# Linear attention and FP4 feed-forward: attention output turned on VectorE and through device memory in place of TensorE

## What is computed

```python
q = _split_heads(x @ Wq); k = _split_heads(x @ Wk); v = _split_heads(x @ Wv)   # 16 heads of 64
q = jax.nn.relu(q) + EPS
k = jax.nn.relu(k) + EPS
context = jnp.cumsum(jnp.einsum('bhnd,bhne->bhnde', k, v), axis=2)
D_inv = 1.0 / jnp.einsum('bhnd,bhnd->bhn', jnp.cumsum(k, axis=2), q)
attn = jnp.einsum('bhnd,bhnde,bhn->bhne', q, context, D_inv)
return attn.transpose(0, 2, 1, 3).reshape(b, n, H * DH) @ Wo + bo
...
x = x + attention(_layernorm(x)); x = x + ffn(_layernorm(x))
```

## Time and profile before

| | us |
|---|---|
| runs, median (lowest to highest) | 1593.6 (1592.9 to 1594.48) |
| profiled execution, span of its instructions | 1592.7 |
| PE busy | 1575.6 |
| DVE busy | 1118.9 |
| ACT busy | 672.7 |
| POOL busy | 477.8 |

### The profile page before, as it was taken

One profiled execution on the slowest core, in us unless ns is written; L12 is line 12 of the kernel. 1 busy time (PEld: TensorE's weight loads), 2 busy tenths in 40 slices (PEclk: granted clock), 3 DMA queues, 4 the chain that ended last, 5 costly groups with the idle time before them and its releaser, 6 DMA issues.

```text
span 1592.7 us, 55490 instructions
## 1 busy us (share of the span) xinstructions
PE 1575.6 (99%) x24464; PEld 1485.6 (93%) x24464; DVE 1118.9 (70%) x2438; ACT 672.7 (42%) x1281; POOL 477.8 (30%) x706
## 2 busy tenths in 40 slices
PE   8999999999999999999999999999999999999998
PEld 6999999999999999999999999999999999999998
DVE  7886766666766667666667666676666666666767
ACT  5444344444444434444344443434434344443433
POOL 3332323323233223232232333222322323322233
PEclk9999999999999999999999999999999999999999
DMA  4100000000000000000000000000000000000000
GB/s 161 33 2 16 16 15 5 15 13 15 15 6 15 12 16 16 15 5 16 12 16 15 6 15 12 16 15 16 5 15 12 16 15 6 15 12 16 9 6 18
DMA packets 22013, 26.82 MB, mean 17 GB/s; under 512 B 1808, under 2 KB 20752, under 8 KB 21776
## 3 DMA queue, kind: packets, MB, share of 16 engines
q1 hardware_dynamic: 21776, 23.27, 4.6%
HBM read 14.88 MB, written 8.39 MB: 15 GB/s over the span
## 4 chain that ended last, share of the span: by engine, by line
PE 94%; DVE 4%; issue 1%; DMA 1%; ACT 0%; SPq 0%; POOL 0%; DVEq 0%; POOLq 0%; ACTq 0%
PE bank L496 66%; PE bank L760 3%; PE bank L629 3%; PE bank L664 3%; PE bank L618 3%; PE bank L580 3%; PE bank L805 3%; PE bank L700 3%; PE bank L727 1%; PE bank L747 1%; PE bank L778 1%; PE bank L602 1%; PE bank L506 1%; DMA qkT<-in_L_attn_Wk 1%; PE bank L739 0%
## 5 line engine op out<-in xcount | busy, mean ns | idle before, releaser
L1011 ACT ACTIVATE qkT<-bank 128x512 f32<-128x512 f32 x256 | 153.0, 599 | 275.9 <-PE bank L496 223.6
L1380 POOL TENSOR_SCALAR qkT<-qkT 128x512 f32<-128x512 f32 x256 | 187.9, 741 | 266.2 <-ACT qkT L1011 266.2
L496 PE MATMUL bank<-xT_hi,wqk_hi 128*128 128x256 f32 x1024 | 213.4, 289 | 0.3 <-DVE wqk_lo L1467 0.3
L496 PE MATMUL bank<-xT_hi,wqk_lo 128*128 128x256 f32 x1024 | 203.1, 279 | 0.0
L496 PE MATMUL bank<-xT_lo,wqk_hi 128*128 128x256 f32 x1024 | 203.1, 279 | 0.0
L1350 POOL TENSOR_TENSOR rstd<-var,minus_half 128x1 f32<-128x1 f32 x64 | 35.6, 556 | 430.3 <-DVE var L1664 430.3
L496 PEld LDWEIGHTS bank<-xT_hi,wqk_hi 128*128 128x128 f32 x1024 | 155.2, 188 | 3.9 <-DVE wqk_lo L1467 0.8
L496 PEld LDWEIGHTS bank<-xT_lo,wqk_hi 128*128 128x128 f32 x1024 | 156.1, 188 | 0.0
L496 PEld LDWEIGHTS bank<-xT_hi,wqk_lo 128*128 128x128 f32 x1024 | 156.0, 188 | 0.0
L1467 DVE TENSOR_TENSOR hqT_lo<-bank,hqT_hi 128x512 fp32r<-128x512 f32 x120 | 63.7, 552 | 118.7 <-ACT hqT_hi L1087 118.7
L1467 DVE TENSOR_TENSOR attnT_lo<-bank,attnT_hi 128x512 fp32r<-128x512 f32 (+1 forms) x128 | 88.0, 689 | 60.8 <-ACT attnT_hi L1078 60.3
(11 more groups left out here) (213 smaller groups left out, 3947.2 us busy)
## 6 DMA issues: line engine op xcount, KB each, us to landing
x_in<-in_L_attn_x SPq DMA_DIRECT2D x32, 256.0 KB, 2.7
out<-out_sb SPq DMA_DIRECT2D x64, 128.0 KB, 1.7
qkT<-in_L_attn_Wq SPq DMA_DIRECT2D x1, 1024.0 KB, 8.7
qkT<-in_L_attn_Wk SPq DMA_DIRECT2D x1, 1024.0 KB, 10.9
probs<-in_L_attn_Wv SPq DMA_DIRECT2D x1, 512.0 KB, 3.5
k_tok<-in_L_attn_Wv SPq DMA_DIRECT2D x1, 512.0 KB, 6.1
attn<-in_L_attn_Wo SPq DMA_DIRECT2D x1, 512.0 KB, 12.1
x<-in_L_attn_Wo SPq DMA_DIRECT2D x1, 512.0 KB, 13.1
```

The lines of the kernel that those rows point to most:

```text
L496: at = pe.matmul(dst, lhs_at(kt), rhs_at(kt), start=first and kt == 0, stop=last and kt == k_tiles - 1)
L1011: act.activation(flat(qkT[:, 2 * m:2 * m + 2, :]), bank[bank_of["qk", c, n]][:], ACT.Relu).then_inc(qk_relu, 1)
L1380: pool.tensor_scalar(at, at, QK_EPS, 1.0, ALU.add, ALU.mult).then_inc(qk_ready, 1)
```

## The change

For chunks 4 to 61 PE no longer turns the attention output. DVE turns it in blocks of 32x32 (`block_attn`, one instruction over 128x1024, from `attn` to `probs`, whose scores are used up by then). Three DMAs store the blocks to device memory (the odd tiles' halves swapped) and four DMAs fetch them back into `attn`, so that the blocks come to lie in turned order. ACT then rounds the tile to the high part in one instruction, and the low part, a subtraction of the whole tile, moves from DVE to POOL. The order of the eight slices in `attnT_hi` changes, and the output product takes them by `attn_slot`.

For even chunks among them (`is_late`) the output product moves to the next step, right behind its attention; with it `add_x`, `variance`, `begin_x`, `end_x` and their partners on ACT and POOL. For odd chunks the product stays at the end of the step, and the high and low parts stand behind the q/k tile n = 5. `mask` now waits until the stores have read `probs`, `normalize` until the low part of the chunk before has read `attn`.

```diff
+    GROUP = 32
+    GROUPS = P // GROUP
+    SENT_ATTN = range(CHUNKS, END)
+        attn_away = nc.dram_tensor("attn_away", (P, INNER), F32, kind="Internal").ap()
...
+        def attn_slot(n, kt):
+            return kt % 2 * (KI // 2) + kt // 2 if n in SENT_ATTN else kt
+        def is_late(n):
+            return n in SENT_ATTN and n % 2 == 0
+        attn_raw = attn[:].rearrange("p (i k c) -> p i k c", i=GROUPS, c=GROUP)
+        attn_blocks = probs[:, 0:INNER].rearrange("p (a o e) -> p a o e", a=GROUPS, o=2)
+        def by_raw_attn(t):
+            return t[:].rearrange("p k (i c) -> p i k c", c=GROUP)
...
+            def send_attn(n):
+                sp.wait_ge(attn_blocks_ready, sent_attn(n) + 1)
+                if sent_attn(n):
+                    sp.wait_ge(attn_back, 16 * GROUPS * sent_attn(n))
+                to = attn_away.rearrange("p (a o e) -> p a o e", a=GROUPS, o=2)
+                sp.dma_start(to[:, :, 0, :], attn_blocks[:, :, 0, :]).then_inc(attn_sent, 16)
+                for half in range(2):
+                    here, there = (slice(DH * k, DH * (k + 1)) for k in (half, 1 - half))
+                    sp.dma_start(to[there, :, 1, :], attn_blocks[here, :, 1, :]).then_inc(attn_sent, 16)
+            def fetch_attn(n):
+                sp.wait_ge(attn_sent, 48 * (sent_attn(n) + 1))
+                at = attn_away.rearrange("(i r) (a e) -> a r i e", r=GROUP, a=GROUPS)
+                for a in range(GROUPS):
+                    sp.dma_start(attn[GROUP * a:GROUP * (a + 1), :].rearrange("r (i e) -> r i e", i=GROUPS), at[a]
+                                 ).then_inc(attn_back, 16)
             def step(b, c):
...
+                if g in SENT_ATTN:
+                    send_attn(g)
+                    fetch_attn(g)
...
                 else:
                     last_attend(b, c, g, u)
+                if is_late(g - 1):
+                    project_out(*divmod(g - 1, CHUNKS), g - 1)
...
-                    turn_attn(b, c, g, n)
+                    if g not in SENT_ATTN:
+                        turn_attn(b, c, g, n)
...
-                project_out(b, c, g)
+                if not is_late(g):
+                    project_out(b, c, g)
...
+            def high_sent_attn(n):
+                act.wait_ge(attn_back, 16 * GROUPS * (sent_attn(n) + 1))
+                act.wait_ge(wo_done, n)
+                act.activation(by_raw_attn(attnT_hi), attn_raw, ACT.Copy).then_inc(attnT_hi_ready, 2)
...
-                if normed:
+                if normed and not is_late(g - 1):
                     normalize_x2(g - 1)
                 evacuate_v(c, u + 1, c % 2, 1 - c // 2)
+                if is_late(g - 1):
+                    high_sent_attn(g - 1)
...
                         relu_qk(c, u + 1, 2 * n)
+                        if n == 0 and is_late(g - 1):
+                            normalize_x2(g - 1)
                         relu_qk(c, u + 1, 2 * n + 1)
+                        if n == 1 and is_late(g - 1):
+                            square_x(g - 1)
...
                         relu_qk(c, u + 1, n)
+                        if n == 5 and c % 2 == 1 and g in SENT_ATTN:
+                            high_sent_attn(g)
...
+            def low_sent_attn(n):
+                pool.wait_ge(attnT_hi_ready, 2 * (n + 1))
+                pool.tensor_tensor(by_raw_attn(attnT_lo), attn_raw, by_raw_attn(attnT_hi).bitcast(F32), ALU.subtract
+                                   ).then_inc(attnT_ready, 2)
...
+                late = is_late(g - 1)
+                if late:
+                    low_sent_attn(g - 1)
...
+                if late:
+                    scale_h(g - 3)
...
+                    add_eps(u + 1, 0)
+                    if late:
+                        rstd_2(g - 1)
+                    for n in range(1, 4):
                         add_eps(u + 1, n)
+                    if late:
+                        scale_x(g - 1)
                     for n in range(4, 6):
                         add_eps(u + 1, n)
+                    if g in SENT_ATTN:
+                        low_sent_attn(g)
...
             def mask(g, n):
+                if n == 0 and g - 1 in SENT_ATTN:
+                    dve.wait_ge(attn_sent, 48 * sent_attn(g))
...
+                if n == 2 and g != LAST:
+                    dve.wait_ge(state_ready, (CHUNKS - 1) * b + c)
...
+                if half == 0 and g - 1 in SENT_ATTN:
+                    dve.wait_ge(attnT_ready, 2 * g)
+            def block_attn(g):
+                dve.wait_ge(attn_ready, 2 * (g + 1))
+                dve.transpose(attn_blocks.rearrange("p a o (k c) -> p o k a c", c=GROUP),
+                              attn[:].rearrange("p (k o a c) -> p o k a c", o=2, a=GROUPS, c=GROUP)
+                              ).then_inc(attn_blocks_ready, 1)
...
                     normalize(g, 0)
                     normalize(g, 1)
+                if g in SENT_ATTN:
+                    block_attn(g)
+                if is_late(g - 1):
+                    add_x(g - 1)
+                    variance(g - 1)
+                if is_late(g - 1):
+                    begin_x(g - 1)
...
+                    if half == 0 and is_late(g - 1):
+                        end_x(g - 1)
+                    if g not in SENT_ATTN:
+                        low_attn(g, half)
...
-                add_x(g)
+                if not is_late(g):
+                    add_x(g)
```

More of the change, by code:

```diff
@@ L206, in build_program @@
         attn_copied, hq_copied = sem("attn_copied"), sem("hq_copied")
+        attn_blocks_ready, attn_sent, attn_back = (
+            sem("attn_blocks_ready"), sem("attn_sent"), sem("attn_back"))
         down_done, out_ready = sem("down_done"), sem("out_ready")
@@ L402, in x2_of, with sent_attn, turned_attn @@
             return x_bias[1][:, 1, :] if n == LAST else x2[:, n % CHUNKS, :]
+        def sent_attn(n):
+            return len(range(SENT_ATTN.start, min(max(n, SENT_ATTN.start), SENT_ATTN.stop)))
+        def turned_attn(n):
+            return n - sent_attn(n)
+        def attn_slot(n, kt):
[6 more added lines that the diff above has]
+            return t[:].rearrange("p k (i c) -> p i k c", c=GROUP)
         def as_rows(t, k):
@@ L767, in project_out @@
                 pe.wait_ge(attnT_hi_ready, 2 * (g + 1))
-                product(dst, lambda kt: attnT_hi[:, kt, :], lambda kt: wo_hi[:, kt, :], KI, first=True)
-                product(dst, lambda kt: attnT_hi[:, kt, :], lambda kt: wo_lo[:, kt, :], KI)
+                product(dst, lambda kt: attnT_hi[:, attn_slot(g, kt), :], lambda kt: wo_hi[:, kt, :], KI, first=True)
+                product(dst, lambda kt: attnT_hi[:, attn_slot(g, kt), :], lambda kt: wo_lo[:, kt, :], KI)
                 pe.wait_ge(attnT_ready, 2 * (g + 1))
-                product(dst, lambda kt: attnT_lo[:, kt, :], lambda kt: wo_hi[:, kt, :], KI, last=True
+                product(dst, lambda kt: attnT_lo[:, attn_slot(g, kt), :], lambda kt: wo_hi[:, kt, :], KI, last=True
                         ).then_inc(wo_done, 1)
@@ L1076, in high_attn @@
             def high_attn(n, half):
-                act.wait_ge(attn_turned, 2 * n + half + 1)
+                act.wait_ge(attn_turned, 2 * turned_attn(n) + half + 1)
                 act.activation(flat(attnT_hi[:, 4 * half:4 * half + 4, :]),
                                flat(turn[bank_of["attn", place(n), half]][:]), ACT.Copy).then_inc(attnT_hi_ready, 1)
+            def high_sent_attn(n):
+                act.wait_ge(attn_back, 16 * GROUPS * (sent_attn(n) + 1))
+                act.wait_ge(wo_done, n)
+                act.activation(by_raw_attn(attnT_hi), attn_raw, ACT.Copy).then_inc(attnT_hi_ready, 2)
             def high_hq(n):
@@ L1157, in step @@
                     square_weights(7)
-                if normed and g != 2:
+                if normed and g != 2 and not is_late(g - 1):
                     square_x(g - 1)
@@ L1180, in step @@
                         silu_of(g - 2, half)
-                    high_attn(g, half)
+                    if g not in SENT_ATTN:
+                        high_attn(g, half)
                 if g == 2:
@@ L1396, in step @@
                     add_bias(0, 0)
-                if exists(g - 1, ALL_CHUNKS):
+                late = is_late(g - 1)
+                if late:
+                    low_sent_attn(g - 1)
+                if exists(g - 1, ALL_CHUNKS) and not late:
                     rstd_2(g - 1)
@@ L1404, in step @@
                         scale_weights((7,))
-                    elif c % 2 == 1 and exists(g - 3, ALL_CHUNKS):
-                        scale_h(g - 3)
                     scale_x(g - 1)
+                if late:
+                    scale_h(g - 3)
                 if g == 3:
@@ L1414, in step @@
                 if project:
-                    for n in range(4):
+                    add_eps(u + 1, 0)
+                    if late:
+                        rstd_2(g - 1)
+                    for n in range(1, 4):
```

(9 more changed lines are left out.)

## The result

| | before | after |
|---|---|---|
| runs, median (lowest to highest), us | 1593.72 (1592.9 to 1594.48) | 1568.71 (1568.09 to 1570.37) |
| span of the profiled execution, us | 1592.7 | 1566.4 |

The time falls by 25.0 us, a ratio of 0.9846 with a 95% interval of 0.9833 to 0.9859. The forecast was 1566 us from a saving of 27.3 us.

What follows compares the result with a forecast made beforehand. PE was taken to bound the kernel, busy for 99% of the span. 51.0 - 11.1 - 12.6 = 27.3 us off the 1592.7 us span gave 1565.4, plus 0.9 for the runs' median: 1566 us, range 1552 to 1597.

Steps and rivals of the forecast that it cites:

- Removed, 51.0 us: PE's eight transposes per chunk, 0.88 us, fall away in 58 chunks: 51.0 us gained.
- c1: Second step of each four-chunk sequence: PE waits for ACT's copy out of bank 7, 0.74 us, 15 times, 11.1 lost.
- c3: Fourth step of a sequence: second q/k product waits for DVE's addition to free bank 3, 0.9 us, 14 times, 12.6 lost.
- no second wait: In c3 the low part is ready at 781.51, before the product's last eight matmuls want it at 781.64: no loss.
- D: Time of DVE's new block transpose, 128x1024, absent from the trace: 1.22 us taken, bounds 0.69 and 2.44.
- The trip: Stores and fetches through device memory, 512 KB each way: 7.4 us, covered by 1.7 us in c3.
- c2: Third step of a sequence, tightest for DVE: residual ends 0.4 us before PE wants the bank for the turned input.
- the second rival: Slow vector side: D = 2.44, c3 loses 1.22 us more, c2 0.8 more: 1594 us, nothing gained; chance 0.20.
- End of odd steps, second norm, no loss: In odd steps POOL's low part and ACT's high part delay nothing PE needs; late second norm has some 15 us.
- The first: Rival: better cover in c3, by a transpose of 0.69 or quicker low part: 12.6 us loss goes, 1554 us; chance 0.10.
- The third: Rival: round trip through device memory becomes the wait of c3; gain gone at 11.1 us, 1607 us at 12; chance 0.12.
- The fourth: Rival: PE stands idle elsewhere for as long, at banks of the hidden tile's transposes: 1590 us; chance 0.08.

Runs made afterwards that it cites:

- the other order: Changed kernel, with DVE doing the late chunk's addition and variance ahead of the block transpose in odd steps, banks unchanged: 1554.31 us, ratio 0.9751.
- the last version: Changed kernel with both moved products in other banks and, in c3, the late product behind the first q/k tile: 1543.27 us, ratio 0.968.
- the move alone: Kernel before, PE turning all chunks and nothing sent, but even chunks' output product and second norm one step later: 1611.97 us, ratio 1.0116.
- The odd chunks alone: Changed kernel, but only the 29 odd chunks 5 to 61 go through device memory and no output product moves: 1567.83 us, ratio 0.9836.

## Why the prediction came out right, and where it was off

- **Removed, 51.0 us: right.** The version with both banks and the later product is 50.9 us below the kernel before.
- **The losses together, 23.7 us: near by offsetting errors.** Of the 51.0 us, 26.0 were lost in the changed kernel's median. The bank in c1 gave 9.4 back where 11.1 were forecast, the bank in c3 12.8 for 12.6, and the product one tile later 4.0 that the prediction put at nothing ("so no second wait").
- **c1, 0.74 us x 15 = 11.1: right.** Row 0.72, 10.7 in all; another bank gave 9.4 back, within the interval.
- **c3, 0.9 x 14 = 12.6: right for the bank, by luck: two terms are off against each other. A second wait was missed.** 0.93 in the trace; another bank gave 12.8, the other order 14.4. But the chain was predicted to start from ACT being through with v. In the trace ACT was through and waited 0.68 us for the DMA. That was partly made up behind it: the high part took 1.07 instead of 1.09, the low part 2.40 instead of 2.56. From the end of v to PE's second q/k tile it is 7.7 us instead of 7.3, and PE itself was later by as much, so that the two errors cancel. PE was later by the wait that the prediction denied: the product's last eight matmuls, wanted at 763.02 + 1.92 = 764.94, started at 765.40, with the low part, 0.46 us late. In most sequences it is less or nothing (the table has 1.1 us in 4). With both banks changed this is what is left, and setting the product one tile later took it away. Of the steps' lengths, three came as predicted (14.34, 32.86, 15.48 for 14.4, 32.9, 15.6); c3 is 32.95 in this sequence for 32.4, with this wait, and 32.64 in the mean (32.11 to 33.23). Against its 31.39 in the last version that is 1.25 us lost each time, not 0.9.
- **D, 1.22 us: right.** 1.246; the bounds of 0.69 and 2.44 were both far off. The Trainium skill, page "VectorE: DVE Perf Modes", section "The three transpose paths", gives 311 ns for a 128x128 tile of bf16; the estimate of 2.5 us for eight of them was twice the measured 1.246 us (float32, one instruction), while the row of a plain DVE operation of as many elements (1.219) was 2% off.
- **The trip, 7.4 us: the mis-sized term.** It took 9.4 here and 9.2 in the mean, and the cover of 1.7 us was none: ACT waited for it in 10 of 14 sequences. The step that failed is the lower bound of each leg, "bound by issue and one last 128 KB", and with it the middle. Its form was right, its numbers weren't: it took 0.33 us for an issue and 1.7 us for the landing from a plain 128 KB store, where these patterns hold SP for 0.53 or 0.64 us (stores) and 0.43 (fetches) and land 2.6 to 3.7 us after the start of their issue. So the stores of this sequence need 5.0 us from the first issue to the last landing, and the four fetches 4.4 more. The upper bound came near by luck (twice 4.7 is 9.4; the prediction writes 9.6): it drew a line of 1.0 us per 128 KB through two rows of different DMAs, but a landing hardly depends on size here (2.6 us for 512, 2.6 for 256, 2.7 for 128 KB), and one store instead of three took just its two issues off. The Trainium skill, page "DMA: Bandwidth & Descriptors", section "Anatomy of one DMA", whose fit is for DMAs that POOL issues, gave an estimated 3.2 us for one transfer of 512 KB; the one store, issued by SP, took 2.6. Its 6.4 us for the trip counts two DMAs where there are seven. The wait of the masks for the stores cost nothing, but with little to spare: the stores landed at 757.25 and the first mask started at 757.42.
- **c2, "the tightest step": the wrong edge.** The residual's slack of 0.4 us was real: the turned input follows it at 757.22, 0.3 us after the residual's end at 756.9, and the move alone showed the wait. But the doubled transpose showed a tighter one, the low parts of the hidden tile ahead of the down product, in both even steps. So the second rival's price, 28 us for a D of 2.44, was too low: with the transpose done twice (2 x 1.25 us) it costs 44, and the time would have been 1613, slower than before and outside the range. With D in its place this didn't count.
- **End of odd steps, second norm, no loss: right.** The odd chunks alone lose nothing, and no PE wait names them.
- **The rivals.** The first (better cover in c3, 1554) didn't happen, and 1555.94 with c3's bank changed is what it would have given. The second fell by D. The third is there as a mechanism, at 0.68 us of ACT's time and with the 4 us of the late low part, not as the outcome. The fourth has nothing left to hold: with the banks and the later product all 51 us are there.

## What to carry to other kernels

When a product is moved past another in an engine's order, look first at which accumulator bank it takes there and at who still has to read it: here two table entries cost 21 of 51 us, and changing them, with one product set one tile later, brought all of it. Put the instruction that frees a bank ahead of work that nobody waits for so soon. And price a trip through memory of this size by its issues, one after another, and the last landing, not by its bytes. The trace's row of the same kind of DMA is the first thing to look for; where there is none, the plan should hold at the upper bound too.

## What the runs showed of the hardware

- **A block transpose costs about what a subtraction of its size costs.** 128x1024 float32 in 32x32 blocks took 1245 to 1249 ns on DVE, all 58 times; the subtraction 1219.
- **DVE stands still beside a long POOL instruction.** The two groups of 128x704 instructions with two SBUF inputs had means of 971 and 980 ns before, 1377 and 1165 after, the longest 3073. The timeline of c1 shows why:

```profile
714.27 2.38 POOL L1395 TENSOR_TENSOR attnT_lo<-attn,attnT_hi 128x1024 fp32r<-128x1024 f32 x1 [11.94 <-ACT attnT_hi L1133]
714.33 3.07 DVE L1590 SCALAR_TENSOR_TENSOR h_scaled<-h_square,h_scaled 128x704 f32<-128x704 bf16 x1
```

  DVE's instruction starts 0.06 us behind POOL's and ends 0.75 us after it, where its median is 0.91: it did next to nothing while POOL's ran. The Trainium skill, page "SBUF — State Buffer", section "SBUF: two separate sides", says that POOL and a DVE instruction with two SBUF inputs share a port pair, which whoever starts first holds for its whole instruction while the other is blocked; the trace agrees. Moving the low part from DVE to POOL thus gave DVE no relief: low parts of 116 x 0.69 = 80 us left it and transposes of 72 us came, yet its busy time rose by 30 us; the two groups alone rose by 37. It is hidden only since PE bounds.
- **A DMA issued right behind the fetches lands later.** The output's stores have the same 128 KB as before. Their landing times, before and after (min/median/max):

```profile
DMA to landing us min/median/max: 1.7/1.7/3.7
...
DMA to landing us min/median/max: 1.7/2.5/4.2
```

  In the sequence shown above, those that SP issues alone (738.95 and 787.38) still land in 1.7 us. The one of 759.05, issued while four fetches are on their way, takes 2.8, and the load of x right behind it 4.7, for 2.7. With the odd chunks alone, where no fetch is on its way at these issues, the medians are 1.8 and 2.8. So it goes by what is in flight, not by the mean traffic (56 GB/s for 17). Nobody waits for these.
